# Two layers chosen by index on one core: A's rows by turns, index words by eight, the fourth pair's first layer in the first pair's banks, the bias spread by TensorE

## The reference

```python
w = weights[subjects]; b = bias[subjects]          # (128,64,64), (128,64)
x = x + einsum('bct,bcd->bdt', x, w) + b[:, :, None]
H = einsum('btd,od->bto', x, W)                    # W is 512 x 512
xa = einsum('btd,brd->btr', x, A[adapter_idx])     # rank 16
delta = einsum('btr,bor->bto', xa, Bm[adapter_idx]) * scalings[adapter_idx]
x = x + H + delta
```

## Time and profile before

| | value |
|---|---|
| median of 3 runs | 244.95 us (244.68 to 245.31) |
| the profiled execution | 244.87 us, span of its instructions 243.2 us |
| PE (matmul) busy | 231.2 us, 95% |
| DVE, ACT, POOL busy | 149.7, 108.8, 73.2 us |
| first matmul of layer 1 | 16.77 us after the span's start |
| DMA | 36.56 MB, mean 150 GB/s |

### The profile page before, as it was taken

How to read it: one execution, slowest core, us unless ns; L and a number is a source line. 1 busy time by engine, 2 the same in 40 slices (tenths; PEclk the granted TensorE clock), 3 DMA queues, 4 the chain that set the end, 5 groups by cost and what they waited for, 6 DMA issues and landing times.

```text
span 243.2 us, 9842 instructions
## 1 busy us (share of the span) xinstructions
PE 231.2 (95%) x2916; PEld 189.1 (78%) x2917; DVE 149.7 (62%) x259; ACT 108.8 (45%) x189; POOL 73.2 (30%) x280
## 2 busy tenths in 40 slices
PE   1989999999999999999999999999999999999991
PEld 1767888888888888888788888888888888888760
DVE  6688866675367836675368736675368754525662
ACT  2175373563526353463525445353526434344431
POOL 3466601560046300651036400656324141000000
...
GB/s 135 265 143 152 160 187 120 213 116 171 152 152 161 140 215 87 202 121 174 159 130 184 128 196 122 189 125 162 161 143 199 94 198 116 201 130 67 84 71 88
DMA packets 23621, 36.56 MB, mean 150 GB/s; under 512 B 6066, under 2 KB 6066, under 8 KB 23602
## 3 DMA queue, kind: packets, MB, share of 16 engines
...
...
## 4 chain that ended last, share of the span: by engine, by line
PE 89%; DVE 5%; DMA 2%; issue 1%; ACT 1%; POOL 0%; SPq 0%; DVEq 0%; ACTq 0%; POOLq 0%
PE ps L859 69%; PE ps L828 13%; PE ps L804 3%; DMA x_ring<-in_x_dram 2%; PE ps L873 1%; PE ps L877 1%; PE ps L763 1%; DVE x_lo L527 1%; DVE m_lo L510 1%; DVE x L519 1%; PE ps L798 0%; DVEq L60 0%; SPq L237 0%; DVE b_parts L491 0%; DVE o_ring L547 0%
## 5 line engine op out<-in xcount | busy, mean ns | idle before, releaser
L859 PE MATMUL ps<-m_hi,x_hi 128*128 x248 | 99.0, 399 | 0.0
L859 PE MATMUL ps<-m_hi,x_lo 128*128 x248 | 96.8, 390 | 0.0
L859 PE MATMUL ps<-m_lo,x_hi 128*128 x248 | 96.7, 390 | 0.0
L527 DVE TENSOR_TENSOR x_lo<-x,x_hi 128x512 fp32r<-128x512 f32 x64 | 44.2, 691 | 62.2 <-ACT x_hi L645 62.0
L368 POOL COPY p_pair<-p_all 64x64 f32 x128 | 40.4, 316 | 124.9 <-DVE x L519 86.6
L645 ACT ACTIVATE x_hi<-x 128x512 fp32r<-128x512 f32 x64 | 40.4, 632 | 54.0 <-ACT o_ring L658 30.0
L658 ACT ACTIVATE o_ring<-ps 128x512 f32<-128x512 f32 x60 | 35.8, 597 | 56.0 <-PE ps L859 55.8
L859 PEld LDWEIGHTS ps<-m_hi,x_hi 128*128 128x128 f32 x248 | 46.5, 188 | 10.4
L859 PEld LDWEIGHTS ps<-m_hi,x_lo 128*128 128x128 f32 x248 | 46.6, 188 | 10.1
L859 PEld LDWEIGHTS ps<-m_lo,x_hi 128*128 128x128 f32 x248 | 46.6, 188 | 9.1
L519 DVE TENSOR_TENSOR x<-ps,bias_pair 128x512 f32<-128x512 f32 x64 | 43.7, 685 | 7.9 <-PE ps L828 7.0
...
## 6 DMA issues: line engine op xcount, KB each, us to landing
x_ring<-in_x_dram SPq DMA_DIRECT2D x124, 128.0 KB, 2.7
out_dram<-o_ring ACTq DMA_DIRECT2D x64, 128.0 KB, 2.7
out_dram<-o_ring SPq DMA_DIRECT2D x64, 128.0 KB, 2.3
a_f<-in_L_cond_A_dram SPq DMA_DIRECT2D x8, 128.0 KB
o_ring<-in_L_cond_W_dram SPq DMA_DIRECT2D x2, 256.0 KB, 4.5
o_ring<-in_L_cond_W_dram ACTq DMA_DIRECT2D x2, 256.0 KB, 5.7
x_ring<-in_x_dram ACTq DMA_DIRECT2D x4, 128.0 KB, 3.2
b_nat<-in_L_cond_Bm_dram ACTq DMA_DIRECT2D x1, 256.0 KB, 3.8
```

Source lines behind the costliest of these rows:

```text
L527: nc.vector.tensor_tensor(x1_lo[:, u % HELD], x1[:, u % 2], x1_hi[:, u % HELD], ALU.subtract).then_inc(x1_lo_ready, 1)
L859: mm = nc.tensor.matmul(ps[:, 2 + u % 2, :], part, m_tile(m, k, c), start=(c == 0 and part is hi and m is m_hi), stop=(c == TC - 1 and par ...
```

## The change

- A is loaded so that its 16 rows lie in turns: row r in four copies on partitions 4r to 4r+3, by a load whose outer dimension is 16 rather than 4. B is copied in the same order (`b_dup`), and `neg` follows: DVE makes it from the bits of the partition number (4 small operations), where POOL made it with 5. POOL takes over the zeroing of the lower half of `a_parts` from DVE.
- `table` is split in `subjects` and `places`; POOL loads eight words for four pairs where it loaded two for each.
- Layer 0 of pair 3 goes to the half banks of pair 0 (`l0_out`, u = 0). It waits for the `x1_add` of pair 0; the `x1_add` of pairs 2 and 3 waits until all four are done.
- The bias comes as one row (2 KB) ahead of Bm on ACT's queue. PE spreads it over the partitions with a row of ones (4 products of 128 columns), ACT copies it to `bias_all`. The load of 256 KB at the end of ACT's queue goes.
- The fourth block of W goes from ACT's queue to SP's.
- `p_all` plus the identity is made on all 128 partitions by two operations of DVE, so that POOL's two copies read the partitions that they write; the wait between these two copies goes.
- The order of DVE and ACT around the first layer 1 is changed, as the rows below show.

The diff, cut to its core:

```diff
@@ loads and tables @@
-        b_dup = sb("b_dup", [P, TC, P // R, R])
+        b_dup = sb("b_dup", [P, TC, P // G, G])
-        p_all = sb("p_all", [C, S, C])
+        p_all = sb("p_all", [P, S, C])
+        bias_row = sb("bias_row", [1, S * C])
-        table = sb("table", [1, PAIRS * 4], I32)
+        places = sb("places", [1, B], I32)
+        subjects = sb("subjects", [1, B], I32)
...
             if isinstance(j, int) and j < L0_QUAD:
-                return j + 1
+                return max(j + 1, L0_QUAD if j > 1 else 0)
...
-        def l0_out(u):
+        def l0_out(j, u):
+            if isinstance(j, int) and j == L0_QUAD - 1:
+                u = 0
@@ SP @@
-            sp.dma_start(w_nat[:, 1, :], W[P:2 * P, :]).then_inc(w_in[1], 16)
+            for o in (1, 3):
+                sp.dma_start(w_nat[:, o, :], W[o * P:o * P + P, :]).then_inc(w_in[o], 16)
...
-                sp.dma_start(a_f[:], A[ds(k, 1)].to_broadcast([G, R, T])).then_inc(a_in, 16)
+                sp.dma_start(a_f[:], A[ds(k, 1)].rearrange("k r t -> r k t").to_broadcast([R, G, T])).then_inc(a_in, 16)
@@ POOL @@
-            nc.gpsimd.memset(neg[:], 0.0).then_inc(consts, 1)
...
+            nc.gpsimd.memset(a_parts[GR:P, :].bitcast(F32), 0.0).then_inc(rows_zeroed, 1)
...
-                s = words(pool, regs, table[0:1, ds(j * 4 + W_SUBJECT, 2)], S - 1)
+                if u % 4 == 0:
+                    pool.load(regs, subjects[0:1, ds(j * 2, 8)])
+                s = [pool.snap(r, min_val=0, max_val=S - 1) for r in regs[2 * (u % 4):2 * (u % 4) + 2]]
...
                 place_p(1)
+                place_p(0)
                 pool.wait_ge(pair_ready, j * 4 + 1)
-                place_p(0)
@@ DVE @@
+            bits = [did(nc.vector.tensor_scalar(bits_i[:, part:part + 1], pid_i[:], 2 - part, None, ALU.bitwise_and))
+                    for part in range(2)]
+            need(bits[1])
+            for part in range(2):
+                nc.vector.tensor_scalar(neg[:, part:part + 1], bits_i[:, part:part + 1], -0.5 - 0.5 * part, None,
+                                        ALU.mult).then_inc(zeroed, 1)
-            nc.vector.memset(a_parts[GR:P, :].bitcast(F32), 0.0).then_inc(zeroed, 1)
...
-            nc.vector.tensor_tensor(p_all[:], p_all[:], ident[0:C, 0:C].unsqueeze(1).to_broadcast([C, S, C]),
-                                    ALU.add).then_inc(p_ready, 1)
+            for side in (1, 0):
+                nc.vector.tensor_tensor(p_all[C * side:C * side + C], p_all[0:C],
+                                        ident[0:C, 0:C].unsqueeze(1).to_broadcast([C, S, C]),
+                                        ALU.add).then_inc(p_ready, 1)
@@ ACT @@
+            act.dma_start(bias_row[:], bias.rearrange("s d -> (s d)").rearrange("(a n) -> a n", a=1)).then_inc(bias_in, 16)
             act.dma_start(b_nat[:], Bm.rearrange("k (p c) r -> p k (c r)", c=TC)).then_inc(bnat_in, 16)
...
+            act.wait_ge(bias_spread, 1)
+            nc.scalar.activation(bias_all[:].rearrange("p s d -> p (s d)"), ps[:, 5, :], ACT.Copy).then_inc(bias_ready, 1)
@@ PE @@
+            def spread_bias(part):
+                cols = slice(part * P, part * P + P)
+                return nc.tensor.matmul(ps[:, 5, cols], ones[0:1, :], bias_row[:, cols], start=True, stop=True)
+            pe.wait_ge(bias_in, 16)
+            for part in range(2):
+                spread_bias(part)
             pe.wait_ge(firsts_ready, 1)
...
+            for part in range(2, TC):
+                mm = spread_bias(part)
+            mm.then_inc(bias_spread, 1)
             pe.wait_ge(place_ready, 1)
...
-                at_least(pe, x1_ready, j - 1)
+                at_least(pe, x1_ready, min(j - 1, 1))
```

More of the change, by code:

```diff
@@ L604, in _ @@
             act.dma_start(scal_row[:], scal.rearrange("(a k) -> a k", a=1)).then_inc(scal_in, 16)
+            act.dma_start(bias_row[:], bias.rearrange("s d -> (s d)").rearrange("(a n) -> a n", a=1)).then_inc(bias_in, 16)
             act.dma_start(b_nat[:], Bm.rearrange("k (p c) r -> p k (c r)", c=TC)).then_inc(bnat_in, 16)
-            for o in range(2, TC):
-                act.dma_start(w_nat[:, o, :], W[o * P:o * P + P, :]).then_inc(w_in[o], 16)
-            act.dma_start(bias_all[:], bias.rearrange("s d -> (s d)").rearrange("(a n) -> a n", a=1)
-                          .to_broadcast([P, S * C]).rearrange("p (s d) -> p s d", s=S)).then_inc(bias_in, 16)
+            act.dma_start(w_nat[:, 2, :], W[2 * P:3 * P, :]).then_inc(w_in[2], 16)
             regs = [act.alloc_register(f"act_word{i}") for i in range(4)]
@@ L902, in step @@
                 else:
-                    k = words(pe, regs[:2 if mixed else 1], table[0:1, ds(j * 4 + W_PLACE, 2 if mixed else 1)], K - 1)
+                    k = words(pe, regs[:2 if mixed else 1], places[0:1, ds(j * 2, 2 if mixed else 1)], K - 1)
                 for i in l0_pairs:
```

74 lines of the change are left out of this document (34 added, 40 removed).

## The result

The changed kernel takes 246.03 us (median of 16 runs) where the kernel before, on the same chip and in turns with it, takes 245.02 (16 runs): a ratio of 1.0043, 95% interval [1.0026, 1.0061]. The forecast was 243.6, range 242.6 to 244.7, with 5 in 100 for slower. It was wrong, in sign too. One run of the changed kernel, at 335 us and a granted clock of 0.67, is disturbed: it is left out of the ratio (without it the median is 245.98).

A forecast was written before the change was run, and what follows sets the result against it. The prediction took PE, busy 95% of the span, to bound the kernel, so the gain was how much earlier Q starts. Terms: -0.35 - 0.4 - 0.55 = -1.3, so 244.87 - 1.3 = 243.6 us, range 242.6 to 244.7.

The forecast's parts named there:

- T0: Start of PE's first layer 0, at 12.79 us in the kernel before; forecast at 12.45.
- Q: The 128 small matmuls (layer 0 of four pairs), starting at 23.93 us before; forecast at 22.6.
- Term 1: Head of the kernel, up to T0: x lands earlier, PE's turning of W then sets T0; -0.35 us.
- I take 0.4 later, near the issue row: Head: the bias row issued ahead of B starts PE's turning of B and W 0.4 us later.
- 0.2 at most: Head: PE's products spreading the bias delay `batch` by at most 0.2 us, within 0.8 us of slack.
- Term 2: From T0 to the end of pair 0 in layer 1: pair 3's new bank lets layer 1 open earlier; -0.4 us.
- Term 3: From pair 1 to Q: DVE's and ACT's new order ends PE's wait for `b_parts`; -0.55 us.
- Q waits again: Rival: Q stays bound by loads of x or POOL's pairs; gain 0.8, 244.1 us; chance 0.14.
- PE's pace rises earlier: Rival: PE's faster clock level comes during the turning of B and W; gain 2.0, 242.9 us; chance 0.13.
- B late by more: Rival: B lands 0.8 to 0.9 us later, T0 stays, Term 2 and Term 3 remain; 243.9 us; chance 0.14.
- Slower: Rival: B, behind `p_all` and in W's traffic, takes 6.0 us and lands 2.65 later; 245.8 us; chance 0.05.
- An idle in PE's run behind Q: Sign of a wrong forecast: PE idle after Q where there was none before; no size given.

The follow-up runs named there:

- e13: The kernel before, with ACT waiting for GpSimd's sixth constant ahead of B's issue, no load added: 246.11 us, ratio 1.0023.
- e1: The changed kernel with the bias loaded to all partitions as before, without row, PE's spread or ACT's copy: 244.06 us, ratio 0.9924.
- e7: The kernel before with only the new order of DVE and ACT and the fourth pair's bank: 244.58 us, ratio 0.9979.
- e4: The changed kernel with B's load ahead of the bias row's, the row spread behind the other small products: 245.32 us, ratio 0.9978.
- e3: The changed kernel with W's fourth block back in ACT's queue: 245.76 us, ratio 1.0003.
- e5: The changed kernel with `p_all` issued behind W's second block: 244.81 us, ratio 0.9983.
- e10: The changed kernel with the bias row issued by SP ahead of W's first block: 244.96 us, ratio 0.9994.
- e9: The kernel before with one more load of 32 bytes, which nobody reads, ahead of B: 246.09 us, ratio 1.0037.
- e14: The kernel before, with ACT waiting for GpSimd's ninth constant ahead of B's issue, no load added: 246.63 us, ratio 1.0038.
- e8: The changed kernel with the bias loaded to all partitions as before and W's fourth block back in ACT's queue: 243.15 us, ratio 0.9919.

## Why the prediction was wrong

**The frame was right.** T0, T0 to Q, and the run behind Q ("Nothing in the change touches that run") add up to the measured difference of the spans: +1.93, -0.76, -0.12.

**Term 1 failed, at one sentence:** "I take 0.4 later, near the issue row". It was -0.35 by forecast and +1.93 by measurement. B's landing moved by 2.0, not 0.4, though its issue moved by 0.3 only. I priced what the added load takes to issue and kept B's 3.8 us from issue to landing as if it were a property of B. It belonged to B's moment among the other loads: issued 0.3 later it is 5.5 (e13). The prediction's upper bound of 0.9 was no bound either, and it even named the mechanism, "behind the small pieces of `p_all`". That the neighbouring W block took 6.0 in the same rows should have been the upper end. The other pieces of the term:
- GpSimd's copy of B took 1.16 and not 0.61 (+0.55): the second `p_all` addition, hidden on DVE as forecast, ran beside it (1.40 us of DVE from 7.91). In the other kernels at most 0.2 of the additions falls beside the copy, and it takes 0.61 to 0.68.
- PE's turning itself is unchanged, 4.63 from the first turned block of B to the last product (4.64 before).
- A by turns does what was said: its load lands 3.4 after its issue, and ACT's rounding of A starts at 9.67 (before 11.41).
- PE no longer waits for x: 0.25 from the last product to T0, where it was 0.92 (-0.67), right in kind.
- GpSimd's copy starts 2.06 later (8.62, before 6.56): 2.06 + 0.55 - 0.01 - 0.67 = 1.93.
- That "0.2 at most" of the spread delays `batch` was wrong as well. The sort came 0.45 earlier (`firsts` at 4.47, before 4.92), but PE's product of it had to wait behind four passes, which took 1.15 us and not half of 1.7, and `batch` came at 7.18, 0.26 later than before. Without the spread (e1) it is at 6.48, so the spread delays it by 0.7. It cost nothing here, since B was later still.

**Term 2 was half as large.** Layer 1 opens at T0 + 3.40 (forecast 3.3, before 3.98), and pair 0 is through at T0 + 6.63 (before 6.84): -0.21 for a forecast of -0.4. Pair 3 doesn't wait, as predicted.

**Term 3 came out as forecast:** from there to Q 3.75 instead of 4.30, -0.55. Both of its parts came: 0.35 of waiting for `b_parts`, and 0.20 from the product to Q. What the prediction missed is on what this rests. It priced A's new load at nothing beyond x, "since A isn't late below either way". With the new order and the old load A is late, by 1.75 us of ACT's time, and the stretch is as long as before (e7). What the words by eight are worth no run shows.

**Q's inputs.** The last `bias_pair` of pair 7 ended at 22.64, over 2 us ahead of Q, so neither it nor x holds Q. The rival "Q waits again" did not come, in this kernel. In e4 Q did wait 0.49 for a load of x.

**The other rivals.** "PE's pace rises earlier" didn't come: PE's turned groups of three take 0.85 to the last, as before, and its 32 first small matmuls 0.79. "B late by more" had the mechanism and stopped at 0.9.

**The rival that came is "Slower",** to which I gave 0.05: B behind `p_all`, terms 2 and 3 kept, 245.8 us. Measured were 2.0 of lateness and 246.03. What spoke for it stood in the rows, and I answered it with "its 3.8 us were measured with W's first block ahead and three behind", which is no reason.

**An idle in PE's run behind Q came after all, a little here and more in the experiments.** The prediction named it as a sign of being wrong. The changed kernel's PE stands idle for 0.27 just behind Q, for nothing that the profile shows (its row is the last one above). In the other kernels with the spread on PE it is 1.22 (e3), 1.14 (e4), 1.36 (e5) and 0.53 (e10). In e3:

```profile
26.41 0.50 PE L877 MATMUL ps<-m_hi,x_hi 128*128 x1
28.12 0.39 PE L877 MATMUL ps<-m_lo,x_hi 128*128 x1 [1.22 <-issue]
```

Of the kernels without the spread, e9 and e14 show 0.23 and 0.27 a few matmuls later, the others none. The "rest" of e3, e4, e5 and e10 is 1.1 to 1.2 longer than the changed kernel's 219.1, which is why they reach Q up to 2.4 us earlier than it and gain much less. In e3, e4 and e5 the idle is most of that, 0.9 to 1.1 more than here. In e10 it is only 0.26 more, and e14's rest is 1.1 longer than before with an idle of 0.27; there the loss is spread over later stretches and I have no cause for it. The spread makes PE's program eight passes longer, and loads of 16 KB in a queue of the kind "instruction" fall near Q (one at 25.2 in e3). That the longer program puts such a load where PE runs out of instructions under the 128 short matmuls is my guess; no run tested it. Against it: e8, with no idle, has such a load between 23 and 24, behind its Q at 22.50, too.
